# Expert blocks of a decoder layer: order of the half-batch normalisation and of the last tile's products

## The chip, the cores and the metric

One core of a Trainium2 chip. The metric is the device time of one execution in microseconds. PE is TensorE, DVE VectorE, ACT ScalarE, POOL GpSimd, SP SyncE. L2205 is line 2205 of the kernel before.

## The reference

Input x is [64, 128, 256] fp32. Three blocks run, each followed by a layer norm of the sum with its input: a selective-scan block, a retention block over a context, and a mixture of experts. The change is in the last one:

```python
shared = einsum('bsi,hi->bsh', silu(x @ shared_gate.T) * (x @ shared_up.T), shared_down)
probs = sigmoid(x @ router_w.T + routing_bias)
scores, indices = top_k(probs, 2); scores = scores / sum(scores)
g = silu(einsum('th,ehi->tei', xf, gate_w))
u = einsum('th,ehi->tei', xf, up_w)
combined = einsum('tei,eih,te->th', g * u, down_w, w)
x = layernorm(x + shared + combined)
```

There are 8 experts, 8192 tokens, two experts per token, 256 columns and 512 hidden ones.

## The kernel before

The first two blocks and the routing take the first 1050 us or so. By then each token's row lies twice in `sorted` in device memory, by expert. The rest of the time is the expert stage, in function `decoder_back`.

**Tiles.** The sorted rows are cut into 71 tiles of 256 (two sub-tiles of 128, `SUBS`), each of one expert. A tile needs a gate and an up product (x by weights, 256 to 512 columns, computed in two parts of 256 hidden columns each), the hidden value h = silu(gate) * up, the down product back to 256 columns, the weighing of each row by its router score, and an adding DMA of each sub-tile into `acc` (sub-tile 0) or `more` (sub-tile 1), indexed by token.

**Split numbers.** To keep fp32 accuracy, every operand of a product is split into a high part, rounded by ScalarE, and a rest, the difference, by VectorE or GpSimd. Weights: `w_high` (ScalarE, L2315) and `w_low` (VectorE, L2680), each twice per tile. Transposed x: L2320 and L2699. Hidden: `high_h` (ScalarE, L2333) and `rest_h` (GpSimd, L2205), each once per part. A product is three passes: high by rest, rest by high, high by high. Twelve matmuls make one part of a gate or up product (L3014); 24 make a tile's down product (L3045).

**Order.** Each engine has a program of its own, written out by hand in a function `tile(i, r, f)`, and the engines meet at semaphores. i is the tile, r its parity and buffer, f a half of the output. TensorE in tile i: gate part 0, up part 0, transposing tile i+1's x, gate part 1, down product of tile i-1, up part 1. The down product waits for both rests of tile i-1's hidden value (`e_h_T_ready`). GpSimd in tile i: rest of part 1 of tile i-1, rest of part 0 of tile i, the two adds of tile i-1, then in odd tiles `half_root`. VectorE in tile i: `times_up` (L2705) of part 1 of tile i-1, `w_low` for tile i+1, `times_up` of part 0, in even tiles `half_bias_of` (L2726), in odd ones `add_half` (L2720), then the second `w_low`, `turn_x` (L2699), `rows` (L2691, L2694: row weights and tokens), in odd tiles `half_moments` (L2732), `weigh` for tile i-1 (L2713, one per sub-tile), in odd tiles `half_means` (L2738).

**Halves of the output.** The output is normalised in 32 halves of 256 rows. From tile 12 on, each pair of tiles (a duo, even then odd) handles one half f, 29 in all. SP loads its rows of `acc` and `more` (`load_half`, L2118) in the even tile once enough adds have landed; in the odd tile VectorE sums them and takes moments and means, and GpSimd takes the reciprocal root of the variance (`half_root`: L2213 adds epsilon, L2215 is the power). In the next even tile VectorE makes the bias, ScalarE normalises (`normalise_half`, L2344) and SP stores. Three late halves are done behind the last tile (`end_moments`, `end_root`, `end_bias_of`, `end_out_of`).

**Last tile.** Tile 70 is even and alone. In TensorE's program it does gate and up part 0, gate part 1, the down product of tile 69, up part 1, and then, outside of `tile`, its own down product. Its last hidden part goes through `times_up` (VectorE), `high_h` (ScalarE) and `rest_h` (GpSimd), all outside of `tile`. SP loads the first late half once all up products are done, and the two others once all adds have landed.

The adds are indirect DMAs, which GpSimd issues itself (L2198):

```python
pool.wait_ge(y_ready, SUBS * i + s + 1)
if not is_at(i, 0):
    pool.wait_ge(added[s], 16 * i)
pool.sem_inc(pool_passed, 1)
pool.indirect_dma_start(...)
```

Of the kernel before, what the change touches and what calls it, by code (L numbers as in the profile page):

```python
# [1767 lines left out]
def decoder_back(nc, d, ps, b, x1_stored):  # L1768
# [3 lines left out]
    with ExitStack() as ctx:  # L1772
# [166 lines left out]
        e_h_T_ready = sem("e_h_T_ready")  # L1939
        row_ready = sem("row_ready")  # L1940
# [212 lines left out]
        def _(pool):  # L2153
# [71 lines left out]
            def tile(i, r, f):  # L2225
                if not is_at(i, 0):
                    rest_h(i - 1, 1 - r, 1)
                rest_h(i, r, 0)
                if not is_at(i, 0):
                    for s in range(SUBS):  # L2230
                        add(i - 1, 1 - r, s)
                if f is not None and r == 1:
                    half_root(f)

            in_tiles(pool, tile)
            rest_h(LAST_TILE, 0, 1)
# [6 lines left out]
        def _(act):  # L2243
# [103 lines left out]
            def tile(i, r, f):  # L2347
                ahead = not is_at(i, LAST_TILE)
                if ahead:
                    w_high(i + 1, 1 - r, 0)  # L2350
                if not is_at(i, 0):
                    high_h(i - 1, 1 - r, 1)
                silu(i, 0)
                if is_at(i, 0):
                    w_down_high(7)
                if ahead:
                    w_high(i + 1, 1 - r, 1)
                    turn_x(i + 1, 1 - r)
                high_h(i, r, 0)
                if is_at(i, 0):  # L2360
                    w_down_high(6)
                silu(i, 1)
                if f is not None and r == 0 and not is_at(f, 0):
                    normalise_half(f - 1)
# [7 lines left out]
            high_h(LAST_TILE, 0, 1)  # L2372
# [4 lines left out]
        def _(dve):  # L2377
# [328 lines left out]

            def weigh(i, r):
# [47 lines left out]
            def tile(i, r, f):  # L2755
# [10 lines left out]
                if f is not None and r == 1:  # L2766
                    add_half(f)
                if ahead:
# [5 lines left out]
                if f is not None and r == 1:  # L2774
                    half_moments(f)
                if not is_at(i, 0):
                    weigh(i - 1, 1 - r)
                if f is not None and r == 1:
                    half_means(f)
# [7 lines left out]
            times_up(LAST_TILE, 1)  # L2787
            weigh(LAST_TILE, 0)
            end_moments(0)
# [10 lines left out]
        def _(pe):  # L2800
# [234 lines left out]

            def down_tile(i, r):
# [13 lines left out]
            def tile(i, r, f):  # L3050
# [4 lines left out]
                gate(i, r, 1)  # L3055
                if not is_at(i, 0):
                    down_tile(i - 1, 1 - r)
                up(i, r, 1)
# [3 lines left out]
            down_tile(LAST_TILE, 0)  # L3062
# [85 lines left out]
```

## Time and profile before

| | us |
|---|---|
| median of 3 runs | 1775.6 |
| lowest and highest | 1774.14, 1776.73 |
| profiled execution, its own time | 1770.39 |
| its span, first to last instruction | 1768.6 |
| its mean granted TensorE clock | 0.983 of full speed |
| PE busy | 1670.3 (94%) |
| DVE, ACT, POOL busy | 1281.5, 914.3, 987.0 |

Everything below comes from that one profiled execution. Times of rows are microseconds from the start of its span. A row of a timeline gives the start, the duration, the engine, the line, the operation with the tensor written and those read, and how many such instructions were merged into it; in square brackets the idle time of the engine before it and what ended that. The chain is the work that ended last, followed back from the last instruction. An engine that is not on it may idle at no cost.

### The profile page before, as it was taken

What the parts mean: (1) busy time and instruction counts of PE and PEld (TensorE: products, weight loads), DVE (VectorE), ACT (ScalarE), POOL (GpSimd) and SP (SyncE); (2) the same over time, 40 slices, a digit from 0 to 9 for tenths busy, and PEclk for the clock granted to TensorE, in tenths of its full rate; (3) what the DMA queues carried; (4) which work ended last, traced back from release to release, by engine and by line L of the source; (5) the groups of instructions that cost most, each with busy time, mean ns of one, the idle gap of its engine ahead of it and who ended that gap; (6) DMA issues with size and microseconds to landing.
All of it is one profiled execution on the core that took longest, in us unless ns stands there. A gap on an engine that the chain in (4) does not pass through costs nothing.

```text
span 1768.6 us, 37723 instructions
## 1 busy us (share of the span) xinstructions
PE 1670.3 (94%) x11030; PEld 1499.6 (85%) x11031; DVE 1281.5 (72%) x2552; ACT 914.3 (52%) x1578; POOL 987.0 (56%) x841
## 2 busy tenths in 40 slices
PE   7999977999979999999999989999999999999994
PEld 6777757899978888888888879999999999999994
DVE  7888867888866667667666676667776777777774
ACT  6888876787633322322322335555555555555552
POOL 2111126888843534534534545777777777777775
PEclk9999998999999999999999999999999999999997
DMA  4555566999935233233233343344444454454544
GB/s 147 185 192 193 194 220 198 255 266 263 297 136 168 97 110 133 94 111 132 94 111 130 109 156 64 60 74 100 99 89 89 100 102 91 91 111 88 96 108 90
DMA packets 149263, 240.78 MB, mean 136 GB/s; under 512 B 40960, under 2 KB 104640, under 8 KB 141008
## 3 DMA queue, kind: packets, MB, share of 16 engines
q1 hardware_dynamic: 122608, 203.58, 36.5%
q0 software_dynamic: 26592, 36.46, 12.1%
q8 instruction: 28, 0.46, 0.1%
q14 instruction: 35, 0.29, 0.1%
HBM read 132.30 MB, written 107.68 MB: 136 GB/s over the span
## 4 chain that ended last, share of the span: by engine, by line
PE 53%; POOL 6%; issue 6%; DVE 3%; DMA 1%; POOLq 0%; ACT 0%; DVEq 0%; SPq 0%; ACTq 0%
PE block_banks L3014 13%; PE block_banks L3045 10%; PE block_banks L2917 6%; PE block_banks L2903 5%; PE block_banks L2894 5%; PE block_banks L2820 5%; POOL more L2198 3%; PE block_banks L2838 2%; POOL back_he_T L2205 2%; PE block_banks L2849 2%; PE block_banks L2857 2%; PE block_banks L2808 1%; DVE back_half_stats L2732 1%; PE block_banks L3007 1%; PE block_banks L2874 1%
## 5 line engine op out<-in xcount | busy, mean ns | idle before, releaser
L3014 PE MATMUL block_banks<-back_xe_T,back_w_split 128*128 128x256 f32 x3408 | 440.0, 286 | 3.0 <-DVE back_w_split L2680 1.5
L3014 PEld LDWEIGHTS block_banks<-back_xe_T,back_w_split 128*128 128x128 f32 x3408 | 420.7, 193 | 3.4 <-DVE back_w_split L2680 1.7
L2205 POOL TENSOR_TENSOR back_he_T<-back_h,back_he_T 128x512 fp32r<-128x512 f32 x142 | 263.0, 1859 | 55.1 <-ACT back_he_T L2333 55.0
L2315 ACT ACTIVATE back_w_split<-back_w_gu 128x1024 fp32r x142 | 150.6, 1061 | 263.0 <-PE block_banks L3014 248.2
L3045 PE MATMUL block_banks<-back_w_down,back_he_T 128*128 x1704 | 223.3, 288 | 31.1 <-POOL back_he_T L2205 31.1
L3045 PEld LDWEIGHTS block_banks<-back_w_down,back_he_T 128*128 128x128 f32 x1704 | 213.4, 195 | 37.1 <-issue 37.0
L2161 POOL DMA_INDIRECT sorted<-back_x,back_slot x128 | 135.6, 1059 | 132.5 <-DVE back_slot L2516 83.7
L2680 DVE TENSOR_TENSOR back_w_split<-back_w_gu,back_w_split 128x1024 fp32r<-128x1024 f32 x142 | 175.5, 1237 | 39.8 <-ACT back_w_split L2315 38.1
L1573 PE MATMUL block_banks<-front_xn_T,front_w_in_parts 128*128 128x512 f32 x768 | 184.6, 395 | 2.5 <-DVE front_xn_T L1344 1.1
L2198 POOL DMA_INDIRECT acc<-back_y,back_token x71 | 112.3, 1582 | 124.3 <-DVE back_y L2713 121.6
L1573 PEld LDWEIGHTS block_banks<-front_xn_T,front_w_in_parts 128*128 128x128 f32 x768 | 141.3, 188 | 39.2 <-DVE front_conv L1337 7.5
L2705 DVE TENSOR_TENSOR back_h<-back_h,block_banks 128x512 f32<-128x512 f32 x142 | 97.7, 688 | 99.0 <-PE block_banks L3014 99.0
L1337 DVE SCALAR_TENSOR_TENSOR front_conv<-block_banks,front_conv_wb,front_conv 128x508 f32<-128x508 f32 (+2 forms) x192 | 140.7, 740 | 33.0 <-ACT front_conv L1121 28.3
L2198 POOL DMA_INDIRECT more<-back_y,back_token x71 | 113.6, 1600 | 22.5 <-issue 22.5
L2917 PE MATMUL block_banks<-back_w_down_s,back_h_T 128*128 128x256 f32 x512 | 115.9, 379 | 1.3 <-DVE back_h_T L2466 1.3
L1726 PE MATMUL block_banks<-front_w_out,front_y_T 128*128 128x256 f32 x512 | 113.2, 379 | 0.0
L2917 PEld LDWEIGHTS block_banks<-back_w_down_s,back_h_T 128*128 128x128 f32 x512 | 95.9, 190 | 14.4 <-DVE back_h_T L2466 1.5
L1726 PEld LDWEIGHTS block_banks<-front_w_out,front_y_T 128*128 128x128 f32 x512 | 96.1, 190 | 12.5
L2327 ACT ACTIVATE back_h<-block_banks 128x512 f32<-128x512 f32 x142 | 83.7, 589 | 44.2 <-POOL back_he_T L2205 28.4
L2300 ACT ACTIVATE back_silu_T<-block_banks 128x512 f32<-128x512 f32 x64 | 38.3, 598 | 131.3 <-PE block_banks L2894 131.2
L1003 POOL TENSOR_SCALAR front_rstd<-front_mean_var 128x4 f32<-128x4 f32 x16 | 3.7, 232 | 183.2 <-DVE front_mean_var L1328 183.2
L2894 PE MATMUL block_banks<-back_x_T,ention_shared_gate_parts 128*128 128x512 f32 x384 | 102.4, 402 | 0.0
(279 smaller groups left out, 3223.1 us busy)
## 6 DMA issues: line engine op xcount, KB each, us to landing
back_xe<-sorted SPq DMA_DIRECT2D x72, 272.0 KB, 2.9
gate_T<-front_gate_T SPq DMA_DIRECT2D x16, 1024.0 KB, 4.9
xc_T<-front_xc_T SPq DMA_DIRECT2D x16, 1024.0 KB, 5.7
front_xc_in<-xc_T SPq DMA_DIRECT2D x16, 1024.0 KB, 7.5
front_gate_in<-gate_T SPq DMA_DIRECT2D x16, 1024.0 KB, 6.1
front_c_rep<-c_parts SPq DMA_DIRECT2D x128, 64.0 KB, 5.4
front_rows_in<-in_x SPq DMA_DIRECT2D x16, 512.0 KB, 8.1
x<-front_x SPq DMA_DIRECT2D x16, 512.0 KB, 3.1
```

What stands on the lines that cost most here:

```text
L1337: nc.vector.scalar_tensor_tensor(out[:, :, lag:], now[:, :, :SEQ_LEN - lag], conv_wb[:, j, D_CONV - 1 - lag:D_CONV - lag], out[:, :, lag:] ...
L1573: op = nc.tensor.matmul(dst[:, j % 2], w_in_parts[:, w_part, k, first * P:(first + 1) * P], xn_T[:, u, x_part, k], start=(n == 0), stop=(n ...
L1726: op = nc.tensor.matmul(out[:, s], y_T[:, ug, j, seq(s)], w_out[:, j], start=(j == 0), stop=(j == KI - 1))
L2161: pool.indirect_dma_start(out=d["sorted"][:, :], out_offset=bass.IndirectOffsetOnAxis(ap=slot[:, u, c, s:s + 1], axis=0), in_=x2[:, u, s], ...
L2198: pool.indirect_dma_start(out=d[("acc", "more")[s]][:, :], out_offset=bass.IndirectOffsetOnAxis(ap=token[:, r, s:s + 1], axis=0), in_=y[:, ...
L2205: nc.gpsimd.tensor_tensor(by_chunk(he_T[:, r, 1], part), h[:, part], by_chunk(he_T[:, r, 0], part).bitcast(F32), ALU.subtract).then_inc(e_ ...
L2315: nc.scalar.activation(w_split[:, r, 0, m].unsqueeze(1), w_gu[:, bass.ds(e, 1), m], ACT.Copy).then_inc(w_high_ready, 1)
L2680: nc.vector.tensor_tensor(w_split[:, r, 1, m].unsqueeze(1), w_gu[:, bass.ds(e, 1), m], w_split[:, r, 0, m].unsqueeze(1).bitcast(F32), ALU. ...
L2894: op = nc.tensor.matmul(ps_wide[:, (2 * i + 2) % 3], w_gate[:, w_part, k, seq(i)], x2_T[:, x_part, k], start=(n == 0), stop=(n == len(PASS ...
L2917: op = nc.tensor.matmul(ps_rows[:, s], h_T[:, i, seq(s)], w_down_s[:, i], start=(i == 0), stop=(i == KF - 1))
L3014: op = nc.tensor.matmul(dst[:, part, c % 2 * WINDOW:(c % 2 + 1) * WINDOW], w_split[:, r, w_part, m, k * D_FF + c * P:k * D_FF + (c + 1) * ...
L3045: op = nc.tensor.matmul(ps_y[:, s, 0:D_MODEL], he_T[:, r, h_part, k, seq(s)], w_down[:, bass.ds(e, 1), w_part, k], start=(n == 0), stop=(n ...
```

## The change

It has three parts. In odd tiles that handle a half, VectorE does the moments and the means right behind the sum, ahead of the second weight rest, and GpSimd does `half_root` ahead of the two adds. In the last tile, TensorE does up part 1 ahead of the down product of tile 69; the multiplication and the high part of the last hidden part move into `tile`; its rest is done by VectorE (`rest_h_end`) with a semaphore of its own, ahead of the weighing of tile 69; and the last down product (`down_last`) is split into a first half of its passes, which needs only hidden part 0, for both sub-tiles, and a second half. Last, VectorE does `end_moments(0)`, the first late half's sum, moments and means, ahead of the weighing of tile 70.

```diff
--- before.py
+++ after.py
@@ -1937,6 +1937,7 @@
         e_h_ready = sem("e_h_ready")
         e_h_high_ready = sem("e_h_high_ready")
         e_h_T_ready = sem("e_h_T_ready")
+        e_end_T_ready = sem("e_end_T_ready")
         row_ready = sem("row_ready")
         y_done = sem("y_done")
         y_ready = sem("y_ready")
@@ -2226,14 +2227,13 @@
                 if not is_at(i, 0):
                     rest_h(i - 1, 1 - r, 1)
                 rest_h(i, r, 0)
+                if f is not None and r == 1:
+                    half_root(f)
                 if not is_at(i, 0):
                     for s in range(SUBS):
                         add(i - 1, 1 - r, s)
-                if f is not None and r == 1:
-                    half_root(f)
 
             in_tiles(pool, tile)
-            rest_h(LAST_TILE, 0, 1)
             for s in range(SUBS):
                 add(LAST_TILE, 0, s)
             for n in range(3):
@@ -2360,6 +2360,8 @@
                 if is_at(i, 0):
                     w_down_high(6)
                 silu(i, 1)
+                if not ahead:
+                    high_h(i, r, 1)
                 if f is not None and r == 0 and not is_at(f, 0):
                     normalise_half(f - 1)
 
@@ -2369,7 +2371,6 @@
                 w_high(0, 0, m)
             turn_x(0, 0)
             in_tiles(act, tile)
-            high_h(LAST_TILE, 0, 1)
             for n in range(3):
                 end_out_of(n)
 
@@ -2704,6 +2705,11 @@
                 dve.wait_ge(e_up_done, 2 * i + part + 1)
                 nc.vector.tensor_tensor(h[:, part], h[:, part], ps_up[:, part], ALU.mult).then_inc(e_h_ready, 1)
 
+            def rest_h_end():
+                dve.wait_ge(e_h_high_ready, 2 * TILES)
+                nc.vector.tensor_tensor(by_chunk(he_T[:, 0, 1], 1), h[:, 1], by_chunk(he_T[:, 0, 0], 1).bitcast(F32),
+                                        ALU.subtract).then_inc(e_end_T_ready, 1)
+
             def weigh(i, r):
                 dve.wait_ge(row_ready, 2 * (i + 1))
                 for s in range(SUBS):
@@ -2765,18 +2771,19 @@
                     half_bias_of(f - 1)
                 if f is not None and r == 1:
                     add_half(f)
+                    half_moments(f)
+                    half_means(f)
                 if ahead:
                     w_low(i + 1, 1 - r, 1)
                     turn_x(i + 1, 1 - r)
                 if is_at(i, 0):
                     w_down_low(6)
                 rows(i, r)
-                if f is not None and r == 1:
-                    half_moments(f)
                 if not is_at(i, 0):
+                    if not ahead:
+                        times_up(i, 1)
+                        rest_h_end()
                     weigh(i - 1, 1 - r)
-                if f is not None and r == 1:
-                    half_means(f)
 
             for m in range(2):
                 w_low(0, 0, m)
@@ -2784,9 +2791,8 @@
             expert_out(GROUPS - 1, 1)
             w_down_low(5)
             in_tiles(dve, tile)
-            times_up(LAST_TILE, 1)
+            end_moments(0)
             weigh(LAST_TILE, 0)
-            end_moments(0)
             end_bias_of(0)
             for n in (1, 2):
                 end_moments(n)
@@ -3033,6 +3039,24 @@
                     pe.wait_ge(base_ready, 2 * GROUPS)
                 project_e(r, 1, ps_up, part).then_inc(e_up_done, 1)
 
+            def down_last():
+                e = pe.value_load(owner[0:1, bass.ds(LAST_TILE, 1)], min_val=0, max_val=EXPERTS - 1)
+                half = len(DOWN_PASSES) // 2
+                for part in range(2):
+                    if part == 0:
+                        pe.wait_ge(e_h_T_ready, 2 * LAST_TILE + 1)
+                    else:
+                        pe.wait_ge(e_end_T_ready, 1)
+                    for s in range(SUBS):
+                        if part == 0:
+                            pe.wait_ge(y_ready, SUBS * (LAST_TILE - 1) + s + 1)
+                        for n, (h_part, w_part, k) in enumerate(DOWN_PASSES[part * half:(part + 1) * half]):
+                            op = nc.tensor.matmul(ps_y[:, s, 0:D_MODEL], he_T[:, 0, h_part, k, seq(s)],
+                                                  w_down[:, bass.ds(e, 1), w_part, k], start=(part == 0 and n == 0),
+                                                  stop=(part == 1 and n == half - 1))
+                        if part == 1:
+                            op.then_inc(y_done, 1)
+
             def down_tile(i, r):
                 e = pe.value_load(owner[0:1, bass.ds(i, 1)], min_val=0, max_val=EXPERTS - 1)
                 pe.wait_ge(e_h_T_ready, 2 * (i + 1))
@@ -3053,13 +3077,16 @@
                 if not is_at(i, LAST_TILE):
                     turn_x(i + 1, 1 - r)
                 gate(i, r, 1)
+                if is_at(i, LAST_TILE):
+                    up(i, r, 1)
                 if not is_at(i, 0):
                     down_tile(i - 1, 1 - r)
-                up(i, r, 1)
+                if not is_at(i, LAST_TILE):
+                    up(i, r, 1)
 
             turn_x(0, 0)
             in_tiles(pe, tile)
-            down_tile(LAST_TILE, 0)
+            down_last()
 
 
 def launch_args(inputs):
```

## Rows read from the trace of the kernel before

**Rows 1.** Waits from 1190 to 1735 us: engine, line, waited for; total, times, longest.

```profile
PE block_banks L3045 <- POOL back_he_T L2205: 26.5, 28, 1.8
```

**Rows 2.** The chain that ended last, in time: start us, us, what.

```profile
1156.40 2.88 PE block_banks L3045 x24
...
1174.55 2.88 PE block_banks L3045 x24
...
1194.51 3.22 PE block_banks L3045 x24
...
1411.40 3.14 PE block_banks L3045 x24
...
1430.57 3.13 PE block_banks L3045 x24
...
1718.98 3.14 PE block_banks L3045 x24
```

**Rows 3.** Busy time by stretch, each engine, then PEclk, DMA share, GB/s.

```profile
1233.90:1238.40 4.50, 4.45 (x24) 4.46 (x25) 2.66 (x5) 1.46 (x3) 2.25 (x2) 0.62 0.63 174
```

**Rows 4.** Timeline of one pair: start, duration, engine, line; idle before in brackets.

```profile
1419.56 0.68 DVE L2720 TENSOR_TENSOR back_half_sum<-back_half_in,back_half_more 128x512 f32<-128x512 f32 x1
...
1420.17 1.21 DVE L2680 TENSOR_TENSOR back_w_split<-back_w_gu,back_w_split 128x1024 fp32r<-128x1024 f32 x1
...
1420.52 2.02 POOL L2205 TENSOR_TENSOR back_he_T<-back_h,back_he_T 128x512 fp32r<-128x512 f32 x1 [0.82 <-ACT back_he_T L2333]
...
1421.90 0.65 DVE L2691 SCALAR_TENSOR_TENSOR back_w_row<-back_columns,back_skipped,back_xe 128x2 f32<-128x2 f32 x1
...
1423.21 0.91 DVE L2713 TENSOR_SCALAR back_y<-block_banks,back_w_row 128x256 f32<-128x256 f32 x2
...
1424.56 1.55 POOL L2198 DMA_INDIRECT acc<-back_y,back_token  x1 [2.01 <-DVE back_y L2713]
...
1426.38 1.28 DVE L2680 TENSOR_TENSOR back_w_split<-back_w_gu,back_w_split 128x1024 fp32r<-128x1024 f32 x1 [0.54 <-ACT back_w_split L2315]
1426.41 1.55 POOL L2198 DMA_INDIRECT more<-back_y,back_token  x1 [0.30 <-issue]
...
1428.12 1.68 PE L3014 MATMUL block_banks<-back_xe_T,back_w_split 128*128 128x256 f32 x12
1428.32 0.72 POOL L2215 TENSOR_TENSOR back_half_rstd<-back_half_rstd,back_neg_half 128x2 f32<-128x2 f32 x1
...
1429.03 3.59 POOL L2205 TENSOR_TENSOR back_he_T<-back_h,back_he_T 128x512 fp32r<-128x512 f32 x2
1429.19 1.12 DVE L2726 SCALAR_TENSOR_TENSOR back_half_bias<-back_half_mean,back_half_rstd 128x2 f32<-128x2 f32 x1 [0.47 <-POOL back_half_rstd L2215]
```

**Rows 5.** Timeline from 1300 to 1318 us, a long add.

```profile
1307.86 1.23 DVE L2680 TENSOR_TENSOR back_w_split<-back_w_gu,back_w_split 128x1024 fp32r<-128x1024 f32 x1 [0.54 <-ACT back_w_split L2315]
1308.03 2.47 POOL L2198 DMA_INDIRECT more<-back_y,back_token  x1 [0.31 <-issue]
...
1309.96 0.83 POOL L2213 TENSOR_SCALAR back_half_rstd<-back_half_mean 128x2 f32<-128x2 f32 x1
```

**Rows 6.** Timeline from 1208 to 1262 us, the sum of a half.

```profile
1221.90 1.03 DVE L2720 TENSOR_TENSOR back_half_sum<-back_half_in,back_half_more 128x512 f32<-128x512 f32 x1
```

**Rows 7.** Timeline of the end, and (last row) the chain there.

```profile
1734.75 2.20 PE L3014 MATMUL block_banks<-back_xe_T,back_w_split 128*128 128x256 f32 x17
...
1751.14 0.68 DVE L2742 TENSOR_TENSOR back_end_sum<-back_end_in,back_end_more 128x512 f32<-128x512 f32 x1
...
1752.65 0.25 DVE L2748 BATCH_NORM_AGGREGATE back_end_mean<-back_end_stats 128x2 f32<-128x6 f32 x2
...
1752.18 3.81 DMA more<-back_y,back_token
```

**Rows 8.** DMA issues: tensors, queue, count, KB each, median us to landing.

```profile
back_half_more<-more SPq DMA_DIRECT2D x29, 256.0 KB, 2.9
...
back_end_more<-more SPq DMA_DIRECT2D x3, 256.0 KB, 4.1
```

## Prediction

> **What bounds the kernel now.** I read the waits of the expert stage first, then the chain of waits, then the timeline of one pair of tiles. From 1190 to 1735 us TensorE waits 28 times, 26.5 us in all, for GpSimd's rest of the hidden tile [rows 1]; the stretch is otherwise filled by matmuls. The chain shows where. Before the output halves come in, the down product (L3045) starts every 18.15 us per pair of tiles (1174.55 - 1156.40). With a half per pair it starts every 19.17 us (1430.57 - 1411.40). Over the 27 pairs from 1194.51 to 1718.98 the sum is 524.47 us, that is 34.4 us more than 27 x 18.15, and the first pair adds 1.8 us (19.96 - 18.15) [rows 2]. So **36.2 us in 28 pairs** is what an end to this stall can bring: 1.02 us in an ordinary pair, more in a few, two of which also lost TensorE's clock: after the long stall the granted clock of the stretch at 1233.9 us was 0.62, so most of it ran at 1.2 GHz and not 2.4, and 24 matmuls filled 4.45 us that take 3.13 else [rows 2, 3].
>
> The timeline tells why. In the odd tile of a pair GpSimd issues add 1 at 1424.56 and add 2 at 1426.41, then does the two root instructions, and only then, at 1429.03, the rest that the down product at 1430.57 waits for; TensorE's last gate product began at 1428.12 and took 1.68, so it was through at 1429.80 [rows 2, 4].
>
> **The change in the loop.** Nothing is added there; two root instructions on GpSimd go ahead of the two adds, and on VectorE the two moments and the two means go from behind the row work to just behind the sum. What matters is where three things then fall: the adds, the weight rest L2680 and the rest L2205.
>
> Root removed from the path: the rest could start 1.6 us sooner (1429.03 less the 1427.4 at which the roots begin, one microsecond behind add 2) if the adds stayed where they are. They do not stay.
>
> VectorE: sum to means takes 1.51 + 0.25 us at the end of the kernel (1751.14 to 1752.65) [rows 7], so L2680 of the odd tile wants to start at 1419.56 + 1.7 = 1421.3 in place of 1420.17. But L2205 then starts first, at 1420.52. The two never overlap in the trace: L2205 at 1420.52 ended 1.16 us after L2680 ended at 1421.38 [rows 4], and the sum L2720 at 1221.90, with an L2205 still running, took 1.03 in place of 0.68 [rows 4, 6]. I take 1.2 us for L2205 alone; it ends at 1421.7, and L2680 then runs to 1422.9. That VectorE, once waiting, goes before GpSimd's next instruction is seen at 1429.19: L2726 waits through the first L2205, and the two L2205 need 3.59 us, not 2.4 [rows 4]: VectorE's L2680 went between them.
>
> Behind L2680 stand x's rest (0.60 us to the next start), the row weights, the tokens and the two weighings. L2691 took 0.65 us, to the very end of L2205 at 1422.54; free, I take 0.15 us for it, and held by GpSimd's power (L2215, 0.72 us [rows 4], started about 1423.3) until 1424.05. The first weighing thus starts between 1423.8 and 1424.2; today it is 1423.21, with the moments ahead of it already. GpSimd does the root while VectorE does this, so the root costs it nothing; its cover is the wait of 2.0 us ahead of add 1. Add 1 comes 1.35 us after the weighing's start (1424.56 - 1423.21), so at 1425.15 to 1425.55, and add 2 1.85 us later (1426.41 - 1424.56), at 1427.0 to 1427.4.
>
> Now the step that decides. L2680 of the even tile starts at 1426.38, set by TensorE and ScalarE, and ends at 1427.6. An add that starts while such an instruction is well under way is held: at 1308.03, 0.17 us behind the L2680 of 1307.86, the add took 2.47 us in place of 1.55 and GpSimd's next instruction came at 1309.96, 2.10 us after that L2680's start [rows 5]. That pattern is there five times in the stage, with add 2 0.17 to 0.72 us behind; with the two starts 0.03 us apart [rows 4], and with the add ahead, it did not. Add 2 at 1427.0 to 1427.4 is inside L2680, so the rest starts at 1426.38 + 2.11 = **1428.49**, 0.54 us sooner than 1429.03. The down product follows 1.54 us later, at 1430.03. An ordinary pair keeps 1.02 - 0.54 = 0.48 us of its excess. The bounds: add 2 not held (next instruction after 1.0 us, from 1428.0 on) leaves next to nothing; the weighing half a microsecond later leaves 0.8. For 28 pairs 28 x 0.48 = 13.4 stay and 22.8 go; I leave 0.8 us for pairs in which add 1 is late for other reasons. **Gain 22 us** (17 to 36). The irregular pairs and the two clock losses are in it: their stall was this same wait of an add, and with a stall near 0.4 us I expect the clock to stay.
>
> The Trainium skill (SBUF — State Buffer, "Who interferes with whom") says that a VectorE instruction with two SBUF inputs shuts out a GpSimd instruction that reads SBUF, and the reverse; by that rule, the trace agrees at L2205 (the 1.16 us above). But the same section infers that generating a DMA's descriptors needs only the write side and so is not held by a tensor-tensor operation. By it add 2 would not be held, which is the first rival; the five held adds speak against it.
>
> What else moves: the weight rest of the odd tile ends 1.5 us later, 1422.9, but its reader, the next tile's up product, starts after 1426; x's rest ends at 1423.6, needed by the gate product at 1424.9: 1.3 us of cover, and if that were gone the loss would be one for one. The second weighing may push L2705 (1425.1) by up to 0.3 us, hidden behind ScalarE, which is busy to 1426.2. SP's loads of a half wait for add 2's landing: up to 1.1 us later, against some 3 us until the sum needs them; SP's load of rows and its store stand behind them, with a whole tile to spare. The half's bias on VectorE no longer waits for the root, but for L2205: same place.
>
> **The change at the end.** TensorE's last gate product ends at 1734.75 + 2.20 = 1736.95 [rows 7]; count from there. Up product moved ahead: 12 matmuls, to 1738.6. VectorE multiplies (0.7), ScalarE copies (I take 0.7), VectorE subtracts (0.7), with three handovers: 1741.0. Behind that instruction on VectorE now stands tile 69's first weighing, so tile 69's add 1 comes only at 1742.3. Its landing, 3.8 us on [rows 7], is before tile 70's add 1, which waits for it. The down product of tile 69 ends near 1741.7, that of tile 70 near 1744.8. But tile 70's weighings now also wait for the first late half: ScalarE normalises half 28 only after the copy, to about 1741.1 (I take 1.1 us for its two instructions), SP stores it and issues the loads at about 1741.6 and 1742.0, and they land 2.9 to 4.1 us later [rows 8]. Add 1.7 us for sum, moments and means: weighing at 1746.6 to 1747.8, add 1 1.3 us later, add 2 1.85 us after that: 1749.7 to 1751.0 against 1752.18 [rows 7]. What follows is the same work. **Gain 1.2 to 2.5, I take 1.9 us**; none if the loads land another 1.3 us late.
>
> **Sum.** The profiled execution took 1770.4 us (span 1768.6); 22 + 1.9 = 24 us less is 1746.4. It was 5.2 us quicker than the median of the runs shown, so the forecast for the median is 1775.6 - 24 = **1751.6 us**, with 1747 to 1759 as this case's own range.
>
> **Rivals.**
> - **Add 2 is not held** (the skill's inference, or a weighing early enough). The rest then starts before 1428.1 and the stall ends: 36.2 + 1.9 = 38 us, **1737.5**. For it: regular adds at 0.03 us distance were not held. Against: all five adds that started later were. Chance 0.15.
> - **The weighing slips.** If the root is long or takes its turn before L2680, VectorE's row work waits, weighing starts at 1424.7 to 1424.9, add 1 at 1426.1, add 2 at 1427.95, the rest at 1428.95: the ordinary stall stays as it is, and only what the long ones and the clock losses add goes (36.2 - 28 x 1.02 = 7.6, perhaps 6). With the end **1768**. For it: the root's first instruction L2213 showed 0.83 us at 1309.96 [rows 5], where I count 0.3, since part of that lay under the add; against: the order at 1429.19. Chance 0.22.
> - **Slower: VectorE is shut out twice.** The place is the odd tile, between L2205 at 1420.52 and add 1. It decides from the point at which add 1 starts after 1426.2, since the rest then starts after 1429.03; each 0.1 us more costs 2.8 us. If L2680 waits for rest and root, and the row weights wait again, add 1 is at 1426.9, the excess 1.74 us in each pair: 28 x 1.74 - 36.2 = 12.5 us lost, 1.9 won: **1786**. Against: the cover of 2 us ahead of add 1 must be used up first. Chance 0.06.
> - My own case has 0.57.
>
> **Numbers.** The range of 8 in 10 runs from 1735 (no stall left) to 1768 (ordinary stalls kept); what is left out is the slower case and the far half of the slip. About 0.2% (3.5 us) is what a measurement of this kernel can tell from no change. Faster: 0.57 + 0.15 + most of 0.22, 0.92. Within: 0.03. Slower: 0.05.
>
> **What would show it.** In the profile after: the period of a pair near 18.6; add 2 of the odd tile at 2.2 us or so in place of 1.55, with GpSimd's next instruction, now L2205, 2.1 us after L2680's start; the root between L2205 and add 1; L2205 of the odd tile short (1.3) and its L2680 long (1.7). TensorE's waits for L2205 near 10 us in total, no clock loss at 1234. At the end, tile 70's weighings right behind the means of the first late half, and the last add at 13 to 14 us after the gate product's end, not 15.2. I am wrong if add 2 is short although it starts inside L2680, or if the weighing of the odd tile starts after 1424.5 in these terms.

## The result, and the profile after

The changed kernel took **1841.2 us** (median; 1839.6 to 1843.9), the kernel before, run beside it, 1774.9: ratio 1.0375, 95% interval 1.0357 to 1.0393. The forecast was 1751.6 us, faster. The profiled execution took 1841.56 us, 71.2 more than the one of before. Rows of after are shown as they answer to those of before.

The chain that ended last in the kernel after: start us, us, what. It answers to [rows 2].

```profile
1155.20 2.88 PE block_banks L3069 x24
1173.35 2.88 PE block_banks L3069 x24
1192.32 3.21 PE block_banks L3069 x24
...
1325.63 5.46 PE block_banks L3069 x24
...
1413.71 3.13 PE block_banks L3069 x24
1435.60 3.14 PE block_banks L3069 x24
...
1787.37 3.13 PE block_banks L3069 x24
```

Up to the first half nothing differs: 18.15 us per pair, and the first pair with a half took 18.97 where before it took 19.96. From then on a pair takes 21.9 us (1435.60 - 1413.71), 2.7 more than before. The 27 pairs to 1787.37 come to 595.05 us, 70.6 more than the 524.47 of before, and that is the result. Three down products, like the one at 1325.63, took 5.46, 4.63 and 5.48 us at a granted clock of 0.51, 0.63 and 0.50, each behind a wait of 3.4 to 3.5 us; 27 pairs of 21.86 us would be 590.2, so these irregular stretches account for some 5 us of the 70.6, and the clock for no more than that.

The waits from 1190 to 1735 us in the kernel after: engine, line, waited for; total, times, longest. They answer to [rows 1].

```profile
POOL acc L2199 <- DVE back_y L2719: 139.8, 48, 3.6
PE block_banks L3069 <- POOL back_he_T L2206: 55.5, 47, 3.5
POOL back_half_rstd L2214 <- DVE back_half_mean L2744: 44.5, 22, 2.0
PE block_banks L3020 <- DVE back_xe_T L2700: 15.6, 21, 0.8
```

TensorE's wait for the rests has doubled and comes in both tiles of a pair, and 21 times it now waits for VectorE as well. The chain's summary on the page has a line that nobody had forecast: the sum of a half, L2726, is 5% of the span. The groups by line from 1190 to 1730 us say by how much (busy us, mean ns of one); first VectorE's two instructions and GpSimd's rests in the kernel before:

```profile
L2726 DVE SCALAR_TENSOR_TENSOR back_half_bias<-back_half_mean,back_half_rstd 128x2 f32<-128x2 f32 x28 | 31.4, 1122 | 18.3 <-POOL back_half_rstd L2215 18.3
L2720 DVE TENSOR_TENSOR back_half_sum<-back_half_in,back_half_more 128x512 f32<-128x512 f32 x28 | 19.5, 697 | 0.0
L2205 POOL TENSOR_TENSOR back_he_T<-back_h,back_he_T 128x512 fp32r<-128x512 f32 x112 | 211.2, 1894 | 22.8 <-ACT back_he_T L2333 22.7
```

The same in the kernel after:

```profile
L2726 DVE TENSOR_TENSOR back_half_sum<-back_half_in,back_half_more 128x512 f32<-128x512 f32 x25 | 79.2, 3170 | 0.0
L2732 DVE SCALAR_TENSOR_TENSOR back_half_bias<-back_half_mean,back_half_rstd 128x2 f32<-128x2 f32 x25 | 76.4, 3057 | 0.0
L2206 POOL TENSOR_TENSOR back_he_T<-back_h,back_he_T 128x512 fp32r<-128x512 f32 x99 | 153.4, 1830 | 3.3 <-ACT back_he_T L2333 3.3
```

A 0.70 us sum has become 3.17 us and a bias of two columns 3.06. The rests tell why. Before, 112 of them at 1894 ns make 212.1 us against 211.2 busy: they hardly overlap. After, 99 at 1830 ns make 181.2 against 153.4 busy: of each two, some 0.56 us lie on top of each other. The timeline of the kernel after, first of the first pair with a half, then of an ordinary pair, which answers to [rows 4]:

```profile
1188.07 1.23 DVE L2681 TENSOR_TENSOR back_w_split<-back_w_gu,back_w_split 128x1024 fp32r<-128x1024 f32 x1 [0.54 <-ACT back_w_split L2315]
...
1189.19 1.55 POOL L2199 DMA_INDIRECT more<-back_y,back_token  x1 [0.30 <-issue]
...
1189.81 1.68 PE L3020 MATMUL block_banks<-back_xe_T,back_w_split 128*128 128x256 f32 x12
...
1190.19 3.10 POOL L2206 TENSOR_TENSOR back_he_T<-back_h,back_he_T 128x512 fp32r<-128x512 f32 x2
1190.33 2.99 DVE L2732 SCALAR_TENSOR_TENSOR back_half_bias<-back_half_mean,back_half_rstd 128x2 f32<-128x2 f32 x1
...
1419.66 1.23 DVE L2681 TENSOR_TENSOR back_w_split<-back_w_gu,back_w_split 128x1024 fp32r<-128x1024 f32 x1 [0.58 <-ACT back_w_split L2315]
1419.80 2.51 POOL L2199 DMA_INDIRECT more<-back_y,back_token  x1 [0.30 <-issue]
...
1421.77 3.08 POOL L2206 TENSOR_TENSOR back_he_T<-back_h,back_he_T 128x512 fp32r<-128x512 f32 x2
1421.88 3.53 DVE L2726 TENSOR_TENSOR back_half_sum<-back_half_in,back_half_more 128x512 f32<-128x512 f32 x1
...
1423.87 3.14 PE L3069 MATMUL block_banks<-back_w_down,back_he_T 128*128 x24 [0.84 <-POOL back_he_T L2206]
...
1426.88 0.22 POOL L2214 TENSOR_SCALAR back_half_rstd<-back_half_mean 128x2 f32<-128x2 f32 x1 [2.03 <-DVE back_half_mean L2744]
...
1427.25 1.23 DVE L2681 TENSOR_TENSOR back_w_split<-back_w_gu,back_w_split 128x1024 fp32r<-128x1024 f32 x1 [0.65 <-issue]
1428.39 0.68 DVE L2700 TENSOR_TENSOR back_xe_T<-block_banks,back_xe_T 128x512 fp32r<-128x512 f32 x1
...
1429.21 3.13 PE L3020 MATMUL block_banks<-back_xe_T,back_w_split 128*128 128x256 f32 x24 [0.76 <-DVE back_xe_T L2700]
...
1430.56 1.62 POOL L2199 DMA_INDIRECT acc<-back_y,back_token  x1 [2.65 <-DVE back_y L2719]
...
1432.48 1.56 POOL L2199 DMA_INDIRECT more<-back_y,back_token  x1 [0.30 <-issue]
...
1433.06 3.56 DVE L2732 SCALAR_TENSOR_TENSOR back_half_bias<-back_half_mean,back_half_rstd 128x2 f32<-128x2 f32 x1
...
1433.49 3.09 POOL L2206 TENSOR_TENSOR back_he_T<-back_h,back_he_T 128x512 fp32r<-128x512 f32 x2
...
1435.60 2.66 PE L3069 MATMUL block_banks<-back_w_down,back_he_T 128*128 x20 [1.35 <-POOL back_he_T L2206]
```

In the ordinary pair the even tile's add 2 starts 0.14 us behind a weight rest and takes 2.51 us (1419.80), and the odd tile's rests come directly behind it. The sum starts at 1421.88 and ends only after both rests have (1421.77 + 3.08 = 1424.85). Now the moments, the root (it waits 2.03 us for the means, and the adds are queued behind it), the weight rest, x's rest (TensorE waits 0.76 us for it) and add 1 all come late; so the next tile's rests are late, again fall directly behind an add, and shut out the bias in its turn. The delay hands itself on: of the 25 sums and the 25 biases of the stretch, 22 each took 2.9 us or more.

What differs between the two orders is seen in the uses of the hidden tile by line (ns min/median/max of one, first and last start). The pair that [rows 4] show, before:

```profile
L2205 POOL TENSOR_TENSOR back_he_T<-back_h,back_he_T x2: 1276/1813/2350, 1429.0 to 1430.3; 128x512 fp32r<-128x512 f32 x2
```

After, the first pair with a half, and an ordinary one:

```profile
L2206 POOL TENSOR_TENSOR back_he_T<-back_h,back_he_T x2: 1844/1856/1869, 1190.2 to 1191.4; 128x512 fp32r<-128x512 f32 x2
...
L2206 POOL TENSOR_TENSOR back_he_T<-back_h,back_he_T x2: 1824/1835/1846, 1421.8 to 1423.0; 128x512 fp32r<-128x512 f32 x2
```

In both kernels the second rest starts 1.2 us behind the first. Before, with the two root instructions between it and the add, the first lasted 1276 ns: the second started as it ended, VectorE's bias got in, and the second rest took 2350 ns. After, a rest directly behind an add lasts 1.85 us, so that the second starts 0.6 us before the first is through.

### The profile page after: what moved, and what is told of

Read it like the earlier page. It is cut to its first block, busy times and chain, and to the rows that moved or that the text cites. A ratio compares the mean times of both kernels' runs of the same rounds, so it can differ in the third digit from the quotient of the medians.

```text
span 1839.7 us, 37723 instructions
## 1 busy us (share of the span) xinstructions
PE 1686.6 (92%) x11030; PEld 1504.0 (82%) x11031; DVE 1382.0 (75%) x2553; ACT 918.5 (50%) x1578; POOL 960.4 (52%) x840
## 4 chain that ended last, share of the span: by engine, by line
PE 45%; DVE 9%; issue 8%; POOL 5%; DVEq 2%; DMA 1%; POOLq 0%; ACT 0%; SPq 0%; ACTq 0%
PE block_banks L3020 10%; PE block_banks L3069 7%; PE block_banks L2923 6%; DVE back_half_sum L2726 5%; PE block_banks L2909 5%; PE block_banks L2900 5%; PE block_banks L2826 4%; POOL more L2199 2%; PE block_banks L2844 2%; POOL back_he_T L2206 2%; PE block_banks L2855 2%; PE block_banks L2863 2%; PE block_banks L2814 1%; DVEq L2686 1%; PE block_banks L2880 1%
## 5 line engine op out<-in xcount | busy, mean ns | idle before, releaser
L3020 PE MATMUL block_banks<-back_xe_T,back_w_split 128*128 128x256 f32 x3408 | 443.6, 285 | 20.5 <-DVE back_xe_T L2700 19.4
L2206 POOL TENSOR_TENSOR back_he_T<-back_h,back_he_T 128x512 fp32r<-128x512 f32 x141 | 223.0, 1813 | 32.8 <-ACT back_he_T L2333 17.7
L2681 DVE TENSOR_TENSOR back_w_split<-back_w_gu,back_w_split 128x1024 fp32r<-128x1024 f32 x142 | 173.8, 1224 | 46.9 <-ACT back_w_split L2315 25.6
L2199 POOL DMA_INDIRECT more<-back_y,back_token x71 | 136.9, 1929 | 23.3 <-issue 21.7
L2333 ACT ACTIVATE back_he_T<-back_h 128x512 fp32r<-128x512 f32 x142 | 88.3, 622 | 38.1 <-DVE back_h L2706 38.1
```

The source lines that it names most:

```text
L2199: pool.indirect_dma_start(out=d[("acc", "more")[s]][:, :], out_offset=bass.IndirectOffsetOnAxis(ap=token[:, r, s:s + 1], axis=0), in_=y[:, ...
L2206: nc.gpsimd.tensor_tensor(by_chunk(he_T[:, r, 1], part), h[:, part], by_chunk(he_T[:, r, 0], part).bitcast(F32), ALU.subtract).then_inc(e_ ...
L2681: nc.vector.tensor_tensor(w_split[:, r, 1, m].unsqueeze(1), w_gu[:, bass.ds(e, 1), m], w_split[:, r, 0, m].unsqueeze(1).bitcast(F32), ALU. ...
L3020: op = nc.tensor.matmul(dst[:, part, c % 2 * WINDOW:(c % 2 + 1) * WINDOW], w_split[:, r, w_part, m, k * D_FF + c * P:k * D_FF + (c + 1) * ...
```

## The experiments

Medians are set against the kernel before, run in turn with each.

**The loop's part alone.** In the kernel before, the moves of root, moments and means:

```diff
                 rest_h(i, r, 0)
+                if f is not None and r == 1:
+                    half_root(f)
...
                     add_half(f)
+                    half_moments(f)
+                    half_means(f)
```

> The kernel before with the loop part of the change alone (moments and means behind the sum, root ahead of the adds). Theory (lock): VectorE's two instructions with two SBUF inputs, the sum and the bias, start under an add and then wait for both of GpSimd's adjacent rests, 3.5 us each; all of the loss is here, so 1840 to 1848 us, pair of tiles 21.9 us. Rival (the end): the loss is in the last tile, then about 1750 to 1775.

Measured 1842.3 against 1772.5: 1.0403 [1.0386, 1.0420]. The whole loss is the loop's.

**The end alone.** The kernel after with these lines put back where they were.

> The kernel after with the loop of before: the last tile's part alone. Lock theory: the loop is back at 19.17 us a pair; the end is worth its own, I expect minus 2 to plus 1 us against before (1773 to 1776). Rival (the end carries the loss): over 1800.

Measured 1771.9: 0.9998 [0.9989, 1.0008]. The end is worth nothing. Its timeline:

```profile
1743.15 0.44 SPq L2132 DMA_DIRECT2D back_end_more<-more  x1
...
1747.99 0.69 DVE L2748 TENSOR_TENSOR back_end_sum<-back_end_in,back_end_more 128x512 f32<-128x512 f32 x1 [5.30 <-DMA back_end_more<-more]
...
1752.78 1.53 POOL L2199 DMA_INDIRECT more<-back_y,back_token  x1 [0.31 <-issue]
```

The load issued at 1743.15 lands 4.8 us later, not the 2.9 to 4.1 I counted, and the weighing of tile 70, now behind that sum, waits for it. Everything in this execution comes 0.68 us later than in the one of before (`times_up` at 1733.42 and 1732.74), so add 2 at 1752.78 answers to 1752.10, against 1752.18 before [rows 7].

**Each half of the loop's part alone.** The expectations call GpSimd's queue closed where its second rest starts in the trace before the first has ended, so that VectorE gets no turn between them, and open where it does. First VectorE's order alone, in the kernel after:

```diff
-                if f is not None and r == 1:
-                    half_root(f)
                 if not is_at(i, 0):
                     for s in range(SUBS):
                         add(i - 1, 1 - r, s)
+                if f is not None and r == 1:
+                    half_root(f)
```

> The kernel after with GpSimd's root back behind the two adds; VectorE keeps moments and means behind the sum. Lock theory: the root stands again between add and rests, so the bias and the sum no longer start under an add; the sum is 0.7 to 1.1 us, the bias 1.1; but weighing and add 1 are some 0.4 us later in the odd tile, so add 2 is held by the weight rest: excess of a pair about 2.1 us and not 1.0, 1790 to 1806 us. Rival (only late moments and means hurt, whatever GpSimd's order): as after, 1840. Rival (only the order of the root hurts): as before, 1775.

Measured 1802.7: 1.0187 [1.0164, 1.0209], as expected. Here the queue stays open (sum 700 ns, bias 1107), but the later weighing puts add 1 4.81 us behind the start of the odd tile's down product, where before it was 4.00, and add 2, 0.85 us behind the weight rest, takes 1.79 us and not 1.55; root and rest come behind it. TensorE waits 49.6 us for L2206, 1.8 per pair. Then GpSimd's order alone: the same diff with its signs turned round, in the kernel before.

> The kernel before with GpSimd's root ahead of the adds and nothing else: VectorE's moments and means stay where they were, so the root waits for means taken behind the weighing, and the adds for the root. Closed-queue theory: adds of the odd tile later than in after, rests right behind a late add, 1835 to 1870 us. Rival (the early moments on VectorE do the harm): 1770 to 1805.

Measured 1842.6 against 1773.1: 1.0386 [1.0369, 1.0404]. GpSimd's order alone is enough for a loss of this size, but not by quite the same road: sum and bias take over 3 us only in every second pair (means 2157 and 1778 ns), and in the pairs between, the adds wait for a root whose means come late, TensorE then waits 3.5 us for the rests, and its down product takes 4.6 us and not 3.1 (the one at 1437.30, granted clock 0.63).

**The bias out of the way.** In the kernel after, the half's bias at the end of the odd tile:

```diff
-                if f is not None and r == 0 and not is_at(f, 0):
-                    half_bias_of(f - 1)
...
+                if f is not None and r == 1:
+                    half_bias_of(f)
```

> The kernel after with the bias of a half moved on VectorE from the middle of the even tile to the end of the odd tile, behind the weighing, where no rest is near. Lock theory: the 3.55 us instruction of the even tile is gone (0.2 us now), the weight rest of the even tile starts 2.5 us sooner, and the even tile loses its stall's cause; the odd tile keeps the shut-out sum. I expect half of the loss back: 1795 to 1820 us. Rival (the root's place in GpSimd's queue makes the adds late, and locks matter little): within 5 us of 1841.

Measured 1839.9: 1.0378 [1.0356, 1.0399]. A miss; the rival's number came out. Its timeline shows who took the bias's place:

```profile
1434.14 4.37 DVE L2681 TENSOR_TENSOR back_w_split<-back_w_gu,back_w_split 128x1024 fp32r<-128x1024 f32 x1 [0.17 <-issue]
1434.33 3.09 POOL L2206 TENSOR_TENSOR back_he_T<-back_h,back_he_T 128x512 fp32r<-128x512 f32 x2
```

The next VectorE instruction with two operands in SBUF is shut out in its place. The weight rest began even 0.19 us ahead of GpSimd's record and still took 4.37 us.

**The sum earlier, too.** As the last, with the sum at the head of VectorE's odd tile, and SP's store of a half ahead of its next load of rows:

```diff
+                if f is not None and r == 1:
+                    add_half(f)
...
-                    add_half(f)
```

> As e4, and the sum of a half moved on VectorE ahead of the first weight rest of the odd tile, out of the window of the two rests; SP stores a half ahead of loading rows. What e4 showed is that the instruction that is shut out is whichever with two SBUF inputs comes next. Theory (closed queue): GpSimd's two rests, issued right behind a late add, leave VectorE no gap, so the second weight rest takes the sum's place and takes over 3 us in the odd tile too; the loss stays mostly, 1815 to 1842 us. Rival (the sum itself was the harm): the odd tile recovers, under 1800.

Measured 1775.0 against 1773.1: 1.0006 [0.9991, 1.0020]. A miss, and again the rival's number: 65 us came back. The odd tile's two rests are apart again, the even one's are not:

```profile
1420.29 1.86 POOL L2206 TENSOR_TENSOR back_he_T<-back_h,back_he_T 128x512 fp32r<-128x512 f32 x1
...
1422.39 1.29 POOL L2206 TENSOR_TENSOR back_he_T<-back_h,back_he_T 128x512 fp32r<-128x512 f32 x1 [0.23 <-ACT back_he_T L2333]
...
1430.42 3.11 POOL L2206 TENSOR_TENSOR back_he_T<-back_h,back_he_T 128x512 fp32r<-128x512 f32 x2
1430.82 3.80 DVE L2681 TENSOR_TENSOR back_w_split<-back_w_gu,back_w_split 128x1024 fp32r<-128x1024 f32 x1 [0.16 <-issue]
```

In the odd tile GpSimd, being early, had to wait 0.23 us for ScalarE before the second rest, and in that gap VectorE was not shut out. The even tile's weight rest still is, for 3.80 us, and the kernel is no slower than the one before: what a shut-out costs depends on what stands behind it.

**The root in the next tile.** In the kernel before, the root behind the rests of the next even tile, where nobody waits for it, and the bias behind that tile's weighings:

```diff
                 rest_h(i, r, 0)
+                if f is not None and r == 0 and not is_at(f, 0):
+                    half_root(f - 1)
```

> The kernel before with GpSimd's root of a half moved into the next even tile, behind both rests, where it waits for y anyway, and the bias behind the weighing there. Closed-queue theory: add 2 of the odd tile is not held (VectorE's order is that of before), the first rest follows it at once and ends 0.4 us before TensorE needs it, the second is not ready by then, so a gap is left: pair of tiles 18.2 us, 1738 to 1748 us. Rival (any rest right behind an add closes the queue): as after, over 1800. Rival (root merely moves its cost): 1770 to 1775.

Measured 1804.2: 1.0171 [1.0146, 1.0196]. A miss, near the rival that any rest right behind an add closes the queue: the rests run through in both tiles (3.09 and 3.08 us for two), the weight rest L2680 took 3.88 us and the sum 3.55. With two instructions shut out in a pair, as in the kernel after, it loses less than half as much: a pair takes 20.5 us (1432.21 - 1411.67). So the shut-outs alone do not make up the loss of after; there the root stands ahead of the adds besides. With the new end as well:

> e6 with the end part of the change as well. With the loop in order the end was worth 0 in e2, so within 2 us of e6, either way. Rival (the end gains once the loop no longer stalls): 3 to 5 us less than e6.

Measured 1807.4: 1.0186 [1.0169, 1.0203]; the end gives nothing here either. With the sum at the head of the odd tile instead, and moments and means behind the weighings:

> e6 with the sum of a half at the head of the odd tile (as in e5) and its moments and means behind the weighing. Nothing of the half then stands ahead of the weighing, so add 1 of the odd tile starts 0.2 us behind the products as in tiles without a half, the root runs where GpSimd waits, and the rests are early, apart and not behind an add. Closed-queue theory: a pair 18.2 to 18.5 us, 1740 to 1752 us. Rival (root and rests on GpSimd are simply too much work, wherever they stand): 1765 or more.

Measured 1771.5 against 1772.8: 0.9992 [0.9981, 1.0003]. A miss: the sum now waits for the store of the previous half, which uses the same tile (73.0 us in 28 waits), and TensorE still waits 28.5 us for the rests.

**The test of the cause: one wait between the two rests.** The kernel after, with nothing moved and one line added on GpSimd:

```diff
                     rest_h(i - 1, 1 - r, 1)
+                    pool.wait_ge(e_h_T_ready, 2 * i)
                 rest_h(i, r, 0)
```

It waits until GpSimd's own first rest has written, so the second cannot be issued under it.

> The kernel after with one wait more on GpSimd: the second rest is issued only once the first has finished (it waits for the first one's own signal). Nothing else differs, and no work is less. Closed-queue theory: VectorE's instruction that waits for the lock now gets in between the rests, so the sum, the bias and the weight rest take under 2.6 us and not 3.5; the loss falls to a third, 1775 to 1805 us. Rival (what matters is that the rests and adds are late, not that they leave no gap): 1838 to 1850.

Measured **1765.8** against 1772.8: 0.9960 [0.9946, 0.9974]. Adding a wait took away 75 us, more than expected. Its timeline:

```profile
1425.28 1.86 POOL L2206 TENSOR_TENSOR back_he_T<-back_h,back_he_T 128x512 fp32r<-128x512 f32 x1
1425.42 1.74 DVE L2733 SCALAR_TENSOR_TENSOR back_half_bias<-back_half_mean,back_half_rstd 128x2 f32<-128x2 f32 x1
...
1427.09 1.21 DVE L2682 TENSOR_TENSOR back_w_split<-back_w_gu,back_w_split 128x1024 fp32r<-128x1024 f32 x1
...
1427.30 2.16 POOL L2206 TENSOR_TENSOR back_he_T<-back_h,back_he_T 128x512 fp32r<-128x512 f32 x1 [0.16 <-POOL back_he_T L2206]
1427.39 3.13 PE L3070 MATMUL block_banks<-back_w_down,back_he_T 128*128 x24 [0.82 <-POOL back_he_T L2206]
```

A gap of 0.16 us lets the bias end with the first rest, and the weight rest goes in ahead of the second, which then takes 2.16 us, as before. The sum is back at 695 ns. TensorE's waits for the rests are 23.8 us in 28 where before they were 26.5, and a pair takes 19.2 us.

**The wait elsewhere.** Added to the kernel with the sum early and the root in the next tile:

> e9 with the same wait. Where the rests are apart anyway it costs nothing: within 2 us of e9, or some us less where e9 still has pairs with a closed queue.

Measured 1771.8: 0.9988 [0.9978, 0.9999]. The wait held GpSimd only twice there, 0.3 us in all, and changes nothing; that the store is the limit in that kernel is read from its waits and was not tested. Added to the kernel before, as a control:

> Control: the kernel before with the same wait between the rests. Its second rest is not issued ahead of the first one's end in ordinary pairs (the first rest takes 1.28 us and VectorE gets in between), so the wait has nothing to open: within 0.2% of before, 1769 to 1777 us. Rival (the wait itself saves time, and e10 beats before by it alone): 1762 to 1768.

Measured 1772.7 against 1774.3: 0.9992 [0.9983, 1.0001]. The wait held GpSimd 28 times, 4.5 us in all, and is worth nothing where the queue is open already: it is not the wait by itself that saves time.

**A version that beats both.** The kernel before with the root and the bias in the next even tile, moments and means both behind the weighings of the odd one, and the wait:

```diff
                     rest_h(i - 1, 1 - r, 1)
+                    pool.wait_ge(e_h_T_ready, 2 * i)
                 rest_h(i, r, 0)
+                if f is not None and r == 0 and not is_at(f, 0):
+                    half_root(f - 1)
...
                     weigh(i - 1, 1 - r)
                 if f is not None and r == 1:
+                    half_moments(f)
                     half_means(f)
+                if f is not None and r == 0 and not is_at(f, 0):
+                    half_bias_of(f - 1)
```

> e6 (root in the next even tile, bias behind the weighing there, the kernel before's end) with moments and means behind the weighing of the odd tile, and with the wait between the two rests of e10. The sum is at its old place, so it doesn't wait for the last half's store as in e9. In e6 the queue closed in both tiles of a pair; the wait should open it. Closed-queue theory: add 1 of the odd tile starts under 1 us behind the products, the first rest ends before TensorE needs it, pair 18.2 to 18.6 us, 1738 to 1755 us. Rival (a rest behind an add costs 0.8 us whatever stands before): 19.2 us a pair, 1765 to 1772.

Measured **1733.4** (1732.3 to 1737.7) against 1774.3: 0.9776 [0.9760, 0.9792], better than expected. Its timeline:

```profile
1408.80 1.55 POOL L2198 DMA_INDIRECT more<-back_y,back_token  x1 [0.30 <-issue]
...
1410.21 1.84 POOL L2205 TENSOR_TENSOR back_he_T<-back_h,back_he_T 128x512 fp32r<-128x512 f32 x1
...
1412.64 1.69 POOL L2205 TENSOR_TENSOR back_he_T<-back_h,back_he_T 128x512 fp32r<-128x512 f32 x1 [0.59 <-ACT back_he_T L2334]
1412.65 3.04 PE L3045 MATMUL block_banks<-back_w_down,back_he_T 128*128 x24
...
1414.60 0.72 POOL L2215 TENSOR_TENSOR back_half_rstd<-back_half_rstd,back_neg_half 128x2 f32<-128x2 f32 x1
...
1421.72 1.48 PE L3045 MATMUL block_banks<-back_w_down,back_he_T 128*128 x11
```

The down product finds its rest ready (one wait is left in the stage, of 3.5 us); a pair takes 18.15 us, as without halves. In this stretch the second rest waits for ScalarE in any case, so the added wait is not what holds it; from 1190 to 1735 us the wait ended no idle time of GpSimd at all.

## Why the prediction was wrong

- **What bounds the kernel** held: 36.2 us lay in this stall. The last version took 1774.3 - 1733.4 = 40.9 us off, and its stall is gone.
- **Where the rest starts** came out once, by luck. TensorE's last gate product starts at 1428.12 before [rows 4] and at 1189.81 in the first pair of after, 238.31 apart, and there the rest starts at 1190.19, which is 1428.50; forecast was 1428.49. But the forecast had add 2 held by the weight rest and the rest 2.11 us behind that one's start. In fact add 2 started 1.12 us behind the weight rest (1189.19 - 1188.07), took 1.55 us, and the rest came 1.0 us behind the add, as in the rival "Add 2 is not held".
- **The first step whose failure cost the gain** is "The down product follows 1.54 us later, at 1430.03". It came 2.13 us later (1192.32 - 1190.19), at 1430.63 in those terms, 0.06 behind the 1430.57 of before. The 1.54 belongs to a rest of 1276 ns behind the root; directly behind an add, where the change puts it, a rest lasts 1.82 to 1.87 us. The step took the record's start for the start of the work: the record starts under the add, and the rest ends 1.3 us behind the add's end (1189.19 + 1.55 = 1190.74 and 1190.19 + 1.85 = 1192.04; in the ordinary pair 1419.80 + 2.51 = 1422.31 and 1421.77 + 1.84 = 1423.61), about the 1.28 us that a rest took behind the root. With the wait added the step is again 2.11 us (1427.39 - 1425.28) and a pair takes 19.2 us, as before: that is what the step is worth, no gain in an ordinary pair. The 7 us by which that kernel beats the one before come with fewer long waits (longest 1.3 us, before 1.8).
- **The step that made the loss** is "That VectorE, once waiting, goes before GpSimd's next instruction is seen at 1429.19". It was seen where the second rest started as the first ended. With the first 0.6 us longer the two overlap and VectorE goes last: 3.0 to 3.6 us for the sum and for the bias, so twice in a pair, and 4.4 for a weight rest when the bias was gone. The wait between the rests gives VectorE its turn again and takes 1841.2 to 1765.8.
- **"The half's bias on VectorE no longer waits for the root, but for L2205: same place"** failed with it: 1122 ns became 3057. When the bias was moved away the weight rest was caught instead, so the bias is where the harm falls and not its cause.
- **Add 2 held by the weight rest**, against the rival "Add 2 is not held": right as a rule, wrong in place. The add that is held is the even tile's: at 1419.80, 0.14 us behind the L2681 of 1419.66, it took 2.51 us. The odd tile's add 2, of which the forecast spoke, took 1.55 us in the first pair and 1.56 in the ordinary one (1432.48), where no weight rest stands beside it. Both signs of being wrong that the prediction named are there: an add 2 that is short although it starts inside the weight rest (1189.19), and, in the ordinary pair, a weighing of the odd tile at 1429.19, 5.32 us behind the start of the down product of 1423.87, where before it was 2.65 us behind (1423.21 - 1420.56). The Trainium skill (SBUF — State Buffer, "Who interferes with whom") infers the opposite for descriptors beside a tensor-tensor instruction; the measurement decides.
- **The end**: right in its order, wrong in the landing. 4.8 us is 0.7 to 1.9 more than the two ends I counted with, the loads were issued 0.4 us later than counted as well (1743.15 less 0.68 is 1742.47, forecast 1742.0), and the step said itself that another 1.3 us would leave nothing.
- **The rivals.** "VectorE is shut out twice" came nearest: right in its sign and in its kind. It failed by place and price: not once in the odd tile with 1.74 us of excess, but in both tiles, each time through two whole rests, with 1.02 + 2.7 = 3.7 us. Its chance of 0.06 was too small, since all that spoke against it beside 2 us of cover was one row, at 1429.19. The same section of the Trainium skill says that the order of issue decides who blocks. Taken at its word, VectorE, waiting since 1421.88, would have gone before a second rest that starts at 1423.0; here it did not.

What stays open: by what rule the turn passes on. That VectorE loses when two GpSimd instructions overlap in the trace, and wins when they don't, is shown; why an overlapping second instruction goes ahead of it is not. That a rest directly behind an add lasts 0.57 us longer because it waits there for the add to end fits the rows above, but no run tests it. How the loss of after divides between the shut-outs and the adds behind the root was not separated. The 1804 and 1733 us versions differ in two things that were not separated either, the place of the moments and the wait; the wait shows no effect in the trace of the second.

## What to carry to other kernels

Small instructions between two large ones of GpSimd can be what gives VectorE its turn: before moving one out, look at each VectorE instruction with two SBUF operands that starts beside what becomes adjacent. Where a rest's or an add's duration is borrowed, borrow it from a row with the same predecessor. And where a loop's period jumps and its waits spread to engines that were idle, look first for one short instruction whose mean has grown several times.

## What the runs showed of the hardware

- GpSimd's next instruction starts in the trace 1.2 us behind a rest of 128x512, whether that one lasts 1.28 or 1.85 us. In the second case a waiting VectorE instruction with two SBUF operands is kept out for both: 3.56 us for a bias of two columns (1433.06, kernel after), 4.37 for a weight rest of 1.23 (1434.14, the bias out of the way).
- A wait on GpSimd's own semaphore between the two costs 0.16 us and opens the turn again.
- An adding DMA that GpSimd issues 0.06 to 1.12 us behind a weight rest on VectorE ended 2.63 to 2.72 us behind that rest's start, whatever the distance, in all 37 cases from 1185 to 1735 us (five before, the others after): it took 2.51 us at 0.14 us behind, 1.55 at 1.12 behind. At 0.02 to 0.04 us behind it took 1.54 to 1.55.
- One load of 256 KB, issued 1.0 us behind the store of a half and beside an adding DMA (the end alone, 1743.15), landed 4.8 us later, where the median of that kind in the loop was 2.9 [rows 8]. Which of the two transfers beside it costs the time was not separated.
